# Weights of nine stages loaded one stage earlier, into their own part of SBUF

## What is computed

```python
x = x + _L0_attn_ref(_layernorm(x, axis=-1), ...)     # a0  16 heads of 8, rotary
x = x + _L0_xattn_ref(_layernorm(x, axis=-1), ctx_1024, ...)   # c0  16 heads of 8, over the context
x = x + _L0_ffn_ref(_layernorm(x, axis=-1), ...)      # f0  feed-forward with chosen low-rank experts
x = x + _L1_attn_ref(_layernorm(x, axis=-1), ...)     # a1, a1n  linear attention, then a norm
x = x + _L1_xattn_ref(_layernorm(x, axis=-1), ctx_1024, ...)   # x1  sliding and iterated attention
x = x + _L1_ffn_ref(_layernorm(x, axis=-1), ...)      # f1  coupled oscillators, three cycles
x = x + _L2_attn_ref(_layernorm(x, axis=-1), ...)     # m1, m2, mj, m3  two state-space passes, join, feed-forward
x = x + _L2_xattn_ref(_layernorm(x, axis=-1), ctx_1024, ...)   # c2  heads of 64, over the context
x = x + _L2_ffn_ref(_layernorm(x, axis=-1), ...)      # f2, g2  16-head attention on chosen rows, gated feed-forward
x = x + _L3_attn_ref(_layernorm(x, axis=-1), ...)     # a3  32 heads of 64
x = x + _L3_xattn_ref(_layernorm(x, axis=-1), ctx_1024, ...)   # c3  16 heads of 8, over the context
x = x + _L3_ffn_ref(_layernorm(x, axis=-1), ...)      # f3  two of eight experts
```

## Time and profile before

| | us |
|---|---|
| median of 3 runs | 7503.16 |
| lowest, highest | 7495.06, 7511.2 |
| the profiled execution | 7525.66 |
| its span, first to last instruction | 7523.9 |
| PE busy | 6564.4 |
| DVE busy | 5422.6 |
| ACT busy | 4148.5 |
| POOL busy | 2881.5 |

### The profile page before, as it was taken

The page is one execution under the profiler, slowest core; times in us unless marked ns, Lnnn a source line. Parts: engine busy times, 40 slices in busy tenths (PEclk is TensorE's granted clock), DMA queues, the critical chain, the costliest instruction groups (busy, mean ns, idle before and its releaser), DMA issues. The chain is left out here.

```text
span 7523.9 us, 190189 instructions
## 1 busy us (share of the span) xinstructions
PE 6564.4 (87%) x74912; PEld 3974.5 (53%) x74912; DVE 5422.6 (72%) x8887; ACT 4148.5 (55%) x6107; POOL 2881.5 (38%) x1663
## 2 busy tenths in 40 slices
PE   7989993887697899978898868989799999989898
PEld 5766671443432333333333345667466676667676
DVE  7877485665457999969999955668567777768444
ACT  4555343665346777767777764556344444456433
POOL 3311183332215888867777801146012222211000
PEclk9999996999898999989999989989999999999999
DMA  1000001000001222212222200000000000000000
GB/s 28 0 18 14 2 0 17 3 3 2 9 0 62 75 75 74 73 57 73 71 73 71 70 3 20 13 2 0 27 6 2 2 2 2 2 14 14 14 0 22
DMA packets 117146, 191.59 MB, mean 25 GB/s; under 512 B 39557, under 2 KB 75562, under 8 KB 116202
## 3 DMA queue, kind: packets, MB, share of 16 engines
q1 hardware_dynamic: 116714, 185.31, 7.8%
HBM read 175.06 MB, written 8.09 MB: 24 GB/s over the span
## 5 line engine op out<-in xcount | busy, mean ns | idle before, releaser
L2480 POOL TENSOR_TENSOR m_dBx<-m_dtx,m_Bs 128x1024 f32<-128x1024 f32 x518 | 1211.1, 2355 | 210.0 <-DVE m_hs L2817 166.9
L2817 DVE TENSOR_TENSOR_SCAN m_hs<-m_ps_dA,m_dBx 128x512 f32<-128x512 f32 x1036 | 1206.7, 1205 | 82.8 <-POOL m_dBx L2480 72.8
L2596 PE MATMUL m_ps_y<-m_yc,ident 128*128 128x512 f32 x2072 | 1073.9, 642 | 0.0
L2689 ACT ACTIVATE m_ps_dA<-m_dt,m_A 128x504 f32<-128x504 f32 x1036 | 687.0, 678 | 499.4 <-DVE m_hs L2817 496.7
L2017 POOL TENSOR_TENSOR a_s<-a_s,a_den 128x1024 f32<-128x1024 f32 x128 | 243.5, 1902 | 1141.4 <-DVE a_den L2063 1141.4
L2828 DVE TENSOR_TENSOR m_yc<-m_hs,m_ps_C 128x1024 f32<-128x1024 f32 x518 | 619.5, 1196 | 2.9 <-PE m_ps_C L2579 2.3
L2596 PEld LDWEIGHTS m_ps_y<-m_yc,ident 128*128 128x128 f32 x2072 | 364.6, 196 | 377.2 <-issue 377.2
L2579 PE MATMUL m_ps_C<-m_parts,m_sel 48*128 48x512 bf16 x520 | 207.1, 398 | 204.7 <-DVE m_yc L2828 204.2
L2579 PEld LDWEIGHTS m_ps_C<-m_parts,m_sel 48*128 48x128 bf16 x520 | 48.3, 93 | 616.4 <-DVE m_yc L2828 458.2
L591 POOL TENSOR_TENSOR c_kbd<-c_kf,c_hmask 128x1024 f32<-128x1024 f32 x66 | 125.0, 1894 | 510.5 <-ACT c_kf L501 486.5
L2061 DVE TENSOR_REDUCE a_den<-a_s 128x16 f32<-128x1024 f32 x128 | 156.0, 1219 | 206.4 <-ACT a_s L1969 206.4
(11 more groups left out here) (748 smaller groups left out, 16156.0 us busy)
## 6 DMA issues: line engine op xcount, KB each, us to landing
m_Bs<-m_BC_rows SPq DMA_DIRECT2D x260, 512.0 KB, 3.6
c_kvb<-in_ctxT SPq DMA_DIRECT2D x68, 128.0 KB, 2.1
c_kvb<-in_ctxT SPq DMA_DIRECT2D x17, 256.0 KB, 2.7
out_dram<-X SPq DMA_DIRECT2D x1, 4096.0 KB
m_BC_rows<-m_low SPq DMA_DIRECT2D x34, 64.0 KB, 2.9
m_part_rows<-m_split SPq DMA_DIRECT2D x34, 48.0 KB, 1.7
m_parts<-m_part_rows SPq DMA_DIRECT2D x34, 48.0 KB, 1.7
m_piece<-m_BC_rows SPq DMA_DIRECT2D x34, 32.0 KB, 1.7
```

Source lines behind the costliest of these rows:

```text
L2480: return nc.gpsimd.tensor_tensor(to, one, other, ALU.mult)
L2596: last = nc.tensor.matmul(ps_y[:, m, :], C.ident[:], of[:, m, :], start=s == 0, stop=s == NS - 1)
L2689: nc.scalar.activation(seqs(ps_dA[:, h % 3, :]), seqs(dt[:, par, m, :]), ACT.Exp, scale=A[:, m, s:s + 1]).then_inc(decay, 1)
L2817: nc.vector.tensor_tensor_scan(hs[:, s % HS, m, :], ps_dA[:, (2 * s + m) % 3, :], dBx[:, s % BX, m, :], 0.0, ALU.mult, ALU.add).then_inc(s ...
```

## The change

A class `Weights` holds the weight tensors of a stage, a semaphore `loaded` and the list of loads. It is allocated before the stages around it, so its tensors lie apart from those of the stage that runs meanwhile. `follow(C, name)` says which stage's weights the next stage is to load, and `load_following(C, sp)` issues them on SP, in the stream of that stage. A `Scope` that is given weights hands out those tensors instead of new ones, and clears their semaphore at its end.

Who loads what: c0 loads f0's weights, f0 a1's, a1n x1's, x1 f1's, f1 m1's, mj m3's, m3 c2's, f2 a3's, and a3 f3's (c3 stands between those two). m2 still loads its own. The waits for `loaded` in the stages stay as they were, with the same counts.

```diff
+def load_following(C, sp):
+
+    if C.following is not None:
+        C.ahead[C.following].start(sp)
...
@@ attn16_table
             for to, of in loads:
                 sp.dma_start(to[:], of).then_inc(loaded, 16)
 
+            load_following(C, sp)
+
             def load(par, at):
...
@@ attn16_linear
         @block.vector
         def _(dve):
             tt, ts = nc.vector.tensor_tensor, nc.vector.tensor_scalar
-            scales.dve(dve)
-            nc.vector.memset(mv[:], 0.0).then_inc(scaled, 1)
-            nc.vector.memset(st[:], 0.0)
             dve.wait_ge(loaded, n_loaded)
             nc.vector.tensor_copy(bv32w[:], bc(bv32[:], [32, P]))
             dve.wait_ge(folded, 1)
             nc.vector.tensor_copy(both[:], ps_s[0:32, 0, 0:D]).then_inc(read, 1)
+            scales.dve(dve)
+            nc.vector.memset(mv[:], 0.0).then_inc(scaled, 1)
+            nc.vector.memset(st[:], 0.0)
             dve.wait_ge(folded, 2)
...
@@ attn64
-            dve.wait_ge(loaded, n_loaded)
             nc.vector.memset(mv[:], 0.0).then_inc(scaled_rows, 1)
+            dve.wait_ge(loaded, n_loaded)
...
@@ focus_block
-            for to, k in loads:
-                sp.dma_start(to[:], W[k]).then_inc(loaded, 16)
             by_tile = ctx_rows.rearrange("(m q) t d -> q t m d", q=8)
             for q in range(8):
                 sp.dma_start(raw_b[q * FT:(q + 1) * FT, :, :], by_tile[q, 0:FT, :, :]).then_inc(rows_in[1], 16)
+            load_following(C, sp)
             sp.wait_ge(x_ready, 2)
```

More of the change, by code:

```diff
@@ L31, in __init__ @@
         self.nc, self.NG, self.NT = nc, groups, groups * TPG
+        self.ahead, self.following = {}, None
         pad = self.NT + 2 * TPG
@@ L42, in __init__, with start @@
         self.ones = sb("ones", [P, P])
+class Weights:
+    def __init__(self, C, ctx, name, shapes, loads, W):
+        self.tensors = {n: ctx.enter_context(C.nc.sbuf_tensor(f"{name}_{n}", shape, F32)) for n, shape in shapes(W).items()}
+        self.loaded = C.nc.alloc_semaphore(name=f"{name}_loaded")
+        self.loads = loads(self.tensors, W)
+        C.ahead[name] = self
+    def start(self, sp):
+        for to, of in self.loads:
+            sp.dma_start(to, of).then_inc(self.loaded, 16)
+def load_following(C, sp):
+    if C.following is not None:
+        C.ahead[C.following].start(sp)
 class Scope:
-    def __init__(self, nc, ctx, name):
+    def __init__(self, nc, ctx, name, weights=None):
         self.nc, self.ctx, self.name = nc, ctx, name
+        self.weights = weights.tensors if weights is not None else {}
         self.sems = []
+        if weights is not None:
+            self.sems.append(weights.loaded)
         ctx.callback(self.clear)
@@ L868, in _ @@
         def _(sp):
-            for to, of in loads:
-                sp.dma_start(to[:], of).then_inc(loaded, 16)
+            load_following(C, sp)
         @block.tensor
@@ L1561, in topk_ffn @@
         block = ctx.enter_context(nc.Block())
-        loads = [(w1[:], W["w1"].rearrange("e d f -> d e f")),
-                 (wr[:], W["wr"]), (falling[:], W["falling"])]
-        loads += [(w2[:, e, :, :], W["w2"][e].rearrange("(c p) d -> p c d", p=P)) for e in range(NE)]
-        n_loaded = 16 * len(loads)
-        @block.sync
-        def _(sp):
-            for to, of in loads:
-                sp.dma_start(to, of).then_inc(loaded, 16)
+        n_loaded = 16 * len(C.ahead[name].loads)
         @block.tensor
@@ L2430, in _ @@
         def _(sp):
-            for to, k in loads:
-                sp.dma_start(to[:], W[k]).then_inc(loaded, 16)
-            sp.dma_start(dt_w[rank_rows, :], W["dt_w"]).then_inc(loaded, 16)
+            if not first:
+                C.ahead[name].start(sp)
             def store_rows(j, par):
@@ L2915, in gelu_ffn @@
         block = ctx.enter_context(nc.Block())
-        loads = [(w1[:], W["w1"]), (w2[:], W["w2"].rearrange("(c p) d -> p c d", p=P)), (b1[:], W["b1"]), (b2[:], bc(W["b2"], [P, D])),
-                 (g[:], W["g"]), (be[:], W["be"])]
-        n_loaded = 16 * len(loads)
+        n_loaded = 16 * len(C.ahead[name].loads)
         @block.sync
         def _(sp):
-            for to, of in loads:
-                sp.dma_start(to, of).then_inc(loaded, 16)
+            load_following(C, sp)
         @block.tensor
@@ L4029, in program, with focus_and_coupled @@
-def program(nc, A, out, groups, which):
+        follow(C, "a1")
+        lora_ffn(C, "f0", f0)
+        follow(C, None)
+        attn16_linear(C, "a1", a1)
+        follow(C, "x1")
+        affine_norm(C, "a1n", A["a1_gamma"], A["a1_beta"])
+def focus_and_coupled(C, A):
+    names = ["w_q", "w_k", "w_v", "w_kh", "w_vh", "w_out", "w_qhT", "w_khT", "b_qh", "b_kh", "b_vh", "lna_g", "lna_b", "lnb_g",
+             "lnb_b", "theta", "temp", "thr", "factor", "base", "place", "hmask", "centre", "mean8", "centre_row", "mean_row",
+             "vmask", "wq_rows", "wk_rows"]
+    x1 = pick(A, "x1_", **{n: n for n in names})
+    names = [f"{k}{n}" for k, m in (("w", 4), ("b", 4), ("gw", 3), ("gb", 3)) for n in range(m)]
+    f1 = pick(A, "f1_", perm="perm", reach="reach", pick="pick_mean", **{n: n for n in names})
+    return x1, f1
@@ new lines, in state_space, with passes @@
+def state_space(C, A):
+    names = ("in_w", "taps", "conv_b", "xp", "dt_w", "dt_b", "A", "D", "out_w", "pick_row", "g", "be")
+    return [pick(A, d + "_", **{n: n for n in names}, **more) for d, more in (("m1", {}), ("m2", {"flip": "flip"}))]
+def passes(C, d, W, first):
+    BC_rows = C.nc.dram_tensor(d + "_BC_rows", (2, 2 * NS, GT), F32, kind="Internal").ap()
+    part_rows = C.nc.dram_tensor(d + "_part_rows", (2, 3, NS * GT), BF16, kind="Internal").ap()
+    mamba(C, d, W, first, BC_rows, part_rows)
```

294 lines of the change are left out of this document (185 added, 109 removed).

## The result

The changed kernel takes 7442.81 us (median of 4 runs, 7436.49 to 7451.69) against 7500.21 for the kernel before measured beside it (median of 4 runs), a ratio of 0.9918 with a 95% interval of 0.9906 to 0.9929. The prediction was 7441. Two later comparisons of the same two kernels gave 0.9928 [0.9911, 0.9945], with medians of 7450.62 and 7512.71, and 0.9925 [0.9911, 0.9938], with 7441.61 and 7500.89.

What follows compares the result with a forecast made beforehand. It took waits for weight DMAs at stage starts, separated by barriers, as the reachable time: 43.3 + 8.3 + 14.5 = 66.1 us gained, 3.7 paid, 62.4 net, from 7503.2 to 7441 us; range 7426 to 7466.

Steps and rivals of the forecast that it cites:

- Starts where one wait goes: Starts of f0, f1, f3, c2, a3, m1 and m3: idle time waiting for weights goes, together 43.3 us.
- a1: Start of a1: the fold starts with the stage and PE turns its first rows 8.3 us earlier; range 6.6 to 9.2.
- The two branches: In a1, scales and ACT's rows end at 912.9, PE's fold and DVE's copies at 913.2; one after the other, 6.6 saved.
- the stretch: In a1, POOL's memset may lengthen DVE's copy of `bv32w` to about 1.1 us; without this, 9.2 us saved.
- x1: Start of x1: context loads follow `xr` directly, so DVE takes the context sums 14.5 us earlier; range 12.5 to 15.4.
- plain following: In x1, context loads straight after `xr`, landing as long after issue as before: sums at 1230.1, 15.4 us saved.
- c0: Start of c0: f0's eight loads ahead of `kvb` delay PE's first key product, costing 3.7 us; range 2.5 to 5.5.
- f2: In f2, `wo` lands behind a3's 5.2 MB just before PE's first scores: cost 0, up to 3 us.
- Less gain: Rival: all lower ends at once, a1, x1, five other starts, c0 and f2, 48.9 us gained, 7454; chance 0.16.
- More gain: Rival: a1 9.2, x1 15.4, c0 2.5, so 65.5 us gained, 7438; below 7428 has chance 0.05.
- it doesn't do what it says: Case of no effect, or of a loss that eats the gain up; chance 0.04.
- SBUF placement slows the scan: Rival: moved tensors slow the state-space scan; 10% more costs 121 us, giving 7562; slower has chance 0.03.

Runs made afterwards that it cites:

- a1_scales_first: Changed kernel with DVE's old order in a1, scales and two memsets ahead of the copies the fold waits for; 7436.91 us, executed once.
- behind_late: Changed kernel with the following stage's loads in attn16_table issued behind the first context pieces and late loads; 7437.7 and 7432.78 us, ratios 0.9909 and 0.9907.
- own_stage: Changed kernel, but each of nine stages issues its own weights at its own start again, SBUF placement kept; 7507.1 us, ratio 0.9998 to the kernel before.
- a1_busy_behind: 33 unused matmuls filling PE's waits in a1's start, on top of the version with following loads behind the late loads; 7455.9 us, executed once.
- changed_3: Third execution of the changed kernel, nothing altered; a1 took 232.2 us, m1 1012.3 and m2 1040.0.

## Why the prediction was right

**Starts where one wait goes.** Said 43.3, measured 43.6. All seven starts behave as computed: what follows the scales stands 0.1 us or less behind them. Read from the second profile of both kernels it is 41.5, 1.3 of the difference by the slow issue in f1.

**a1.** Said 8.3, measured 8.7. The two branches run beside each other and the fold's is the later, by 0.5 us. The copy `both` ended 913.50 - 912.35 = 1.15 us after the barrier, where the prediction had 1.4; the copy in front of it took 1.10 us beside POOL's memset, as it had said, and 0.21 us in a1_scales_first, where it came after that memset. The upper bound of 9.2 without the stretch doesn't follow from the prediction's own numbers: 0.95 + 3.0 us behind the start gives 8.8.

**x1.** Said 14.5, measured 14.4; the sums of the context were put at 18.8 us and came at 18.9. The step that could have failed, eight context loads behind eight `xr` loads, held: in the changed kernel the sixteen land one after the other, about 1 us apart, the last of `xr` 11.6 and the last of the context 18.9 us after the barrier. The issue of the context loads took 4.54 us, longer than before but less than the bound had it. The 0.9 us that the prediction added to plain following was its choice and no reading, so the last 0.1 us of agreement is luck; the later profiles had the sums up to 0.6 us later.

**c0.** Said 3.7, measured 3.8 at the start (up to 4.1 in later profiles) and 4.1 over the stage. behind_late shows the cause: eight issues ahead of the context. It is none of the data: the first piece of the context landed 2.1 us after its own issue in the changed kernel and 2.2 in the kernel before.

**f2.** Said 0 with up to 3; it is 1.2 at the scores and 3.1 over the stage. The step that failed is the end of a3's loads. The prediction took them from the earlier trace rows, 17.7 us, and had `wo` land at 21.2 us after the barrier. The landings in the changed kernel put the last of them 19.2 us after the first issue, and `wo` at 22.7 us. Why the same seven loads take longer in f2 than at a3's own start is open; it is not their place in the queue, since they took 19.3 us behind `wo` in behind_late too, and 18.0 at a3's start in own_stage. The mechanism (queue behind 5.2 MB) is shown by the three versions in which `wo` stands ahead of all, of 1 MB, or of none of them. The Trainium skill has a rule on this, that on each DMA engine the descriptors of a queue are consumed in the order of the ring (DMA: Bandwidth & Descriptors, section on queues, rings and completion order). The trace agrees: `wo` takes 2.0 us to land ahead of a3's loads and 15.3 behind them.

The other 1.9 us come after the scores, and the prediction had no term for them. The window of 7 us that begins 30 us after f2's barrier shows where: first the kernel before, then the changed one, then the second profile of the kernel before, with the granted clock third from the end.

```profile
4978.50:4985.50 7.00, 6.60 (x56) 3.74 (x56) 4.80 (x8) 4.03 (x6) 4.91 (x9) 0.76 0.00 1
```

```profile
4921.60:4928.60 7.00, 5.66 (x41) 2.78 (x42) 4.76 (x7) 2.56 (x3) 3.71 (x8) 0.51 0.00 1
```

```profile
4945.70:4952.70 7.00, 6.71 (x50) 3.70 (x51) 4.68 (x7) 3.61 (x5) 5.01 (x9) 0.63 0.00 1
```

The third shows that a lower clock there costs nearly as much without late scores: its scores started at 21.5 us, and still f2 took 334.3, 1.5 us more than the 332.8 of the first, at 0.63 instead of 0.76 (a1_busy_behind, with 0.61, took 334.6). With the late scores f2 took 335.8 to 336.0 in all five profiles, even where they came at 23.8, so the 1.2 and the 1.9 are not two costs that add up for every delay.

**Less or more than the sum.** The three ratios, 0.9918, 0.9928 and 0.9925, stand for 61, 54 and 56 us off 7503.16; the medians beside them differ by 57.4, 62.1 and 59.3 us. The sum said 62.4, which is 0.9917 and lies within all three intervals, so no shortfall is shown. The forecast of 7441 against 7442.81 is nearer than the method can be, and partly luck. The prediction and the column of the starts share one profile of the kernel before, with its slow issue in f1; read from the second profile of each kernel, the starts gain 64.2 us, pay 5.4 and give 58.8. And a start is not the whole stage: f2 pays 1.9 us more than its start shows, and f0 keeps about 1.0 us less than its 2.4 in two of three profiles.

**The rivals.** Less gain (7454) was the nearest: it had f2 at 3 and c0 at 5.5, of which the first came true over the stage, but a1, x1 and the five starts lost little or nothing. More gain did not come. That it doesn't do what it says, and that SBUF placement slows the scan, are refuted: the scan took 1203 ns after and 1205 before, and own_stage lies at the kernel before.

```profile
L2903 DVE TENSOR_TENSOR_SCAN m_hs<-m_ps_dA,m_dBx 128x512 f32<-128x512 f32 x1036 | 1205.7, 1203 | 84.4 <-POOL m_dBx L2566 76.3
```

**A sign that misled.** "I am wrong if the loops of c0, m1 or a3 change by more than that, or if the sum of the differences at the starts isn't the difference of the spans." By that, the first profile would have refuted me: m1 changed by 17.2 and the spans by 74.0. The prediction took its profile's span, 22.5 us above the median, as a constant that would cancel. It doesn't: m1 was 16.8 us longer than in a second profile of the same kernel, where the granted clock was higher, m2 8.0 and x1 6.5 longer, while a3 was 7.0 shorter. The median escaped this only because the forecast subtracted its terms from it and used no difference of spans.

## What to carry to other kernels

Where stages end in a barrier, the idle time in front of the first dependent instruction of each stage can be read and added up, and a load moved one stage forward returns it up to what comes second there: nearly all in seven of the nine starts here, 14.4 of 23.3 us in x1. That second-latest thing has to be found for each start. Issue such loads behind everything that the running stage itself loads: each one ahead costs its issue time (0.47 us), and megabytes ahead of a small load delay it by their whole transfer. Compare stages counted from their own barrier, in two profiles of each kernel, before a difference of spans is explained; a wait for a DMA, too, is read from two profiles, since here it moved by up to 1.3 us between them.

## What the runs showed of the hardware

- One execution of the same instructions differs from another, by 24.5 us between the spans of the two profiles of the kernel before and by up to 44 us between its plain executions, and the granted clock goes with it: 0.947 at 7523.9 and 0.950 at 7499.4 us for the kernel before, 0.952 at 7449.9 and 0.955 at 7435.6 for the changed one. The prediction had the loops repeating to a few microseconds. The Trainium skill says that one and the same kernel starts with a different number of slow matmuls from run to run (TensorE: Matmul & The Clock Gate, section What's actually happening). The traces show the same at the start of a stage: in a1's first 33 us PE got through 340 matmuls in one profile of the changed kernel and 467 in another. And they show that it isn't only the start: the granted clock over the whole stage m1 was 0.95 in one profile of the kernel before and 0.97 in the next.
- Now and then SP takes longer over the issue of one load. The first two loads at the start of g2 took 0.80 us to issue before and 1.81 in the first profile of the changed kernel, and g2 was 2.4 us longer. One load of g2 was as slow in changed_3 (1.3 us, g2 159.7) and in own_stage (1.6 us, g2 161.2); in the ten other profiles none was, and g2 took 158.8 to 159.1. The slow issue in f1 of the kernel before (1.7 us for one load) is of the same kind. What delays it is open.
- In x1, sixteen loads issued back to back within 11.4 us landed about 1 us apart, with the DMA share above 1.
